# Row transfers by GpSimd in pairs, each pair waiting for the one before it to land

## The reference

```python
x = x + L0_conv(_gn(x))        # deformable 3x3 convolution
x = x + L1_conv(_gn(x))        # attention over the 1024 positions, 16-wide keys
t = _to_tokens(x)
t = t + L2_attn(_ln_t(t))      # attention with a distance bias
t = t + L2_ffn(_ln_t(t))       # mixture of 8 experts, top 2 of them
t = t + L3_attn(_ln_t(t))      # 16-head linear attention
t = t + L3_ffn(_ln_t(t))       # mixture of 8 experts, top 2 of them
```

```python
top2_vals, top2_idx = jax.lax.top_k(probs, 2)
...
h = gelu(xf @ w1 + bb1); y = h @ w2 + bb2
acc + we[:, None] * y
```

## Time and profile before

| | |
|---|---|
| median of 3 executions | 2342.63 us (2340.99 to 2352.11) |
| profiled execution, first to last instruction | 2532.1 us |
| mean granted TensorE clock in it | 0.883 of full speed |
| PE, DVE, ACT, POOL busy in it | 1926.7, 1494.0, 1039.0, 555.5 us |

### The profile page before, as it was taken

One profiled execution on the slowest core, in us unless ns is written; L12 is line 12 of the kernel. 1 busy time (PEld: TensorE's weight loads), 2 busy tenths in 40 slices (PEclk: granted clock), 3 DMA queues, 4 the chain that ended last, 5 costly groups with the idle time before them and its releaser, 6 DMA issues.

```text
span 2532.1 us, 35891 instructions
## 1 busy us (share of the span) xinstructions
PE 1926.7 (76%) x10992; PEld 1518.5 (60%) x10992; DVE 1494.0 (59%) x3449; ACT 1039.0 (41%) x1773; POOL 555.5 (22%) x535
## 2 busy tenths in 40 slices
PE   4777878887688777877778876786778877768749
PEld 1665656566556565756646665565656666556636
DVE  2356545876357754777447763577547864485363
ACT  3134144525363162733546253642627335443323
POOL 0000112021213323032222312133230422232020
PEclk7889989988899889988889888998889988888969
DMA  7901952474446734584455844476344844431410
GB/s 250 198 1 42 210 150 76 110 170 136 123 137 162 199 101 127 146 184 142 117 145 158 187 138 122 135 178 182 101 132 146 192 132 126 128 122 55 129 35 9
DMA packets 259912, 337.51 MB, mean 133 GB/s; under 512 B 29552, under 2 KB 191840, under 8 KB 259424
## 3 DMA queue, kind: packets, MB, share of 16 engines
q1 hardware_dynamic: 243648, 297.70, 44.7%
q0 software_dynamic: 14336, 29.39, 4.2%
q10 hardware_dynamic: 1696, 7.66, 0.8%
HBM read 267.56 MB, written 67.08 MB: 132 GB/s over the span
## 4 chain that ended last, share of the span: by engine, by line
PE 33%; issue 19%; DVE 18%; ACT 6%; DVEq 5%; DMA 5%; SPq 4%; another core or an unknown queue 4%; POOL 3%; ACTq 2%; PEld 0%; PEldq 0%; POOLq 0%
PE pair L948 5%; PE pair L1067 4%; POOL gotten L808 2%; PE pair L935 2%; PE pair L1235 2%; PE pair L1225 2%; PE pair L1115 2%; DMA dist<-hats 2%; PE pair L1127 2%; PE pair L1075 2%; DVE dist L1642 2%; PE pair L861 2%; PE pair L881 2%; DVE nmax L1751 1%
## 5 line engine op out<-in xcount | busy, mean ns | idle before, releaser
L948 PE MATMUL pair<-dist,thirds 128*128 128x256 f32 (+6 forms) x1440 | 299.2, 360 | 66.7 <-DVE dist L1642 60.7
L948 PEld LDWEIGHTS pair<-dist,thirds 128*128 128x128 f32 x1440 | 259.5, 205 | 115.3 <-DVE dist L1642 61.2
L1067 PE MATMUL pair<-vt,dist 128*128 128x128 f32 x2048 | 270.7, 288 | 37.3 <-DVEq L1745 32.9
L1067 PEld LDWEIGHTS pair<-vt,dist 128*128 128x128 f32 x2048 | 256.2, 202 | 60.5 <-DVEq L1745 49.8
L1433 ACT ACTIVATE hidden_sb<-pair,wring 128x128 f32<-128x128 f32 x644 | 184.3, 367 | 234.8 <-PE pair L1115 135.2
L808 POOL DMA_INDIRECT gotten<-ys,row x224 | 226.0, 1009 | 128.1 <-issue 65.8
L1115 PE MATMUL pair<-turned_sb,wring 128*128 128x128 f32 x1288 | 193.1, 295 | 65.1 <-DVEq L1796 37.2
L1127 PE MATMUL pair<-wring,hidden_sb 128*128 128x128 f32 x1288 | 184.5, 288 | 71.6 <-DVE tnF L1764 35.9
L1115 PEld LDWEIGHTS pair<-turned_sb,wring 128*128 128x128 f32 x1288 | 172.8, 205 | 106.6 <-DVEq L1796 61.9
L1642 DVE TENSOR_TENSOR dist<-dist,prob 128x1024 f32<-128x1024 f32 x144 | 173.9, 1224 | 95.7 <-DMA dist<-hats 46.9
L1127 PEld LDWEIGHTS pair<-wring,hidden_sb 128*128 128x128 f32 x1288 | 169.3, 202 | 81.7 <-issue 65.8
(11 more groups left out here) (256 smaller groups left out, 3162.0 us busy)
## 6 DMA issues: line engine op xcount, KB each, us to landing
dist<-hats SPq DMA_DIRECT2D x576, 128.0 KB
wring<-wa SPq DMA_DIRECT2D x161, 321.0 KB
wring<-wb SPq DMA_DIRECT2D x161, 321.0 KB
prob<-hats SPq DMA_DIRECT2D x288, 128.0 KB
hats<-dist SPq DMA_DIRECT2D x40, 512.0 KB, 3.9
ys<-by SPq DMA_DIRECT2D x70, 256.0 KB, 2.3
blocks_sb<-xs SPq DMA_DIRECT2D x28, 512.0 KB, 6.7
blocks_sb<-xs SPq DMA_DIRECT2D x14, 448.0 KB, 8.0
```

The source lines that it names most:

```text
L948: last = pe.matmul(pair[0][:, a:b], z[k // 3 % 2][:, c, k % 3, :], rhs(a, b), start=bank not in opened, stop=final, skip_group_check=True)
L1067: last = pe.matmul(psum[bank][:, 0:P], prT[j % 2][:, t, :], vt[:, t, :], start=(t == 0), stop=(t == NT - 1))
```

## The change

In `send` and `fetch` every part but the first now waits until all the parts before it have landed. With `part` counting from 0, each part before it has added 32 to the semaphore, hence the `32 * part`; `at(m, 256, ...)` counts the images before. And the last three parts of scatter A move from hooks 36, 44, 44 to 46, 47, 48, behind the `gn1` root at 45 and the second gating-B root at 46. No other table changes.

```diff
-SEND_A_AT = [28, 32, 34, 34, 36, 36, 44, 44]
+SEND_A_AT = [28, 32, 34, 34, 36, 46, 47, 48]
...
                 if part == 0:
                     pool.wait_ge(sem(f"routed{l}"), at(m, 1, 1))
                     pool.sem_inc(sem("moves_begun"), 1)
+                else:
+
+                    pool.wait_ge(sem(f"sent{l}"), at(m, 256, 32 * part))
                 tn = which(l)[3]
                 for r, j in MOVES[2 * part:2 * part + 2]:
                     pool.indirect_dma_start(xs[l], ...)
...
                     pool.sem_inc(sem("moves_begun"), 1)
+                else:
+
+                    pool.wait_ge(sem(f"got{l}"), at(m, 256, 32 * part))
                 for r, j in MOVES[2 * part:2 * part + 2]:
                     pool.indirect_dma_start(got[r][:, j, :], ...)
```

## The result

The changed kernel takes 2489.0 us at the median of 4 executions, the kernel before, run beside it on the same chip, 2345.07 us. The ratio is 1.0612, with a 95% interval of 1.0581 to 1.0642: **144 us slower**. The forecast was a rise of 58 us to 2401 us, with a range of 2320 to 2470 us. The direction was right; the size was not, and the time lies beyond the range.

What follows compares the result with a forecast made beforehand. The prediction took the kernel as bound by chains running from engine to engine, no engine being full. Its terms, 21 + 15 + 14 + 8 = 58 us, on 2342.6 us gave 2401 us, range 2320 to 2470 us.

Steps and rivals of the forecast that it cites:

- The price of one wait: In GpSimd's list, one wait on a landing adds 1.84 us, up to 3.60 us.
- Part one: Scatter A, group norm's root: TensorE's blocks 4.5 to 7.5 us late; 3 us in 7 periods, 21 us.
- Part two: Scatter B, second layer norm's root: GpSimd 3.3 us late without the stop; 2.5 us in 6 periods, 15 us.
- Part three: Gather A: VectorE's first settle waits 4.3 us without a stop; half let through, 2 us in 7 periods, 14 us.
- Part four: Gather B: ends far ahead of its use, covered by the convolution; costed at nothing.
- Part five: The end, behind the last period: less side work to fill a wait; 8 us, 26 us at most.
- The first: Rival: the stops are part of every execution and the pauses end them; 2241 us, chance 0.18.
- The second: Rival: everything is hidden by the covers; about 2343 us, within 0.5%, chance 0.14.
- The third: Rival: landings slow everywhere, each wait 3.60 us; 127 us more, 2470 us, chance 0.08.
- The stops: VectorE's waits ending with "remote" inside GpSimd's bursts, 159.3 us; taken to belong mostly to the profiled execution.

Runs made afterwards that it cites:

- experiment 2: Against the kernel before: waits only in scatter A, with its three pairs moved as in the changed kernel; 2378.59 us, ratio 1.0155.
- experiment 6: Against the kernel before: scatter A's three pairs moved, without any wait; 2359.11 us, ratio 1.0058.
- experiment 4: Against the kernel before: waits only in gather A, old order of steps; 2394.67 us, ratio 1.0206.
- experiment 8: Against the kernel before: waits only in the last five of the 28 bursts (35 waits), old order; 2390.81 us, ratio 1.0190.
- experiment 1: The kernel before, unchanged, run again for a second profile; 2345.42 us, ratio 1.0024, profiled span 2342.9 us.
- experiment 10: Against the kernel before: only every second pair waits (three waits a burst instead of seven), old order; 2365.79 us, ratio 1.0080.

## Why the direction was right and the size was not

**The mechanism** was right: pauses in GpSimd's list cost nothing by their sum, and they cost where another engine's step stands behind them. Every sign that the forecast named is in the profile after: pairs further apart (4.80 us in scatter B, forecast about 4.4), the group norm's root released by VectorE, a load of the blocks 13.0 us behind the second gating root (1149.75 to 1162.76; forecast about 12), TensorE's new wait for it, the second layer norm's root right behind a transfer, the first settle waiting for the gather.

**The price of one wait** was too low: 1.84 us was taken, 2.34 us is the mean, and it depends on the place: 13.4 us for six waits ahead of scatter B's root (1227.82 - 1196.78 against 1169.23 - 1151.64), 2.24 us each; 15.9 us for seven in gather A, 2.27 each; 3.3 us in gather B (3.6 - 0.3); 1.2 us in most waits of the last scatter (1.53 - 0.30). The forecast took the lower price "as most bursts stand in the attention stretches", as if these were quiet; scatter B and gather A stand there, and their waits are the 2.24 and 2.27 us. For the quiet stretch the sum was too high instead: landing and restart were added up to 1.29 + 0.85 = 2.14 us and took 1.53 us together. In the changed kernel the price goes with the traffic: the DMA share is 0.11 in the quiet last scatter (2274 to 2290), 0.48 and 0.52 in the scatter B and gather A shown, 0.91 in a gather B (1060 to 1111). That the traffic is the cause was not tested.

**Part one** forecast that TensorE finds the blocks 4.5 to 7.5 us late and let 3 us of it through: 21 us. The lateness was right (5.26 us in the period shown, 34.3 / 7 = 4.9 in experiment 2). The allowance for VectorE's slack was wrong: by itself the part cost 34 us, all of the lateness, and some 16 of them come with the move alone (experiment 6), for which the forecast's terms give 0 to 10 us. Beside the other waits TensorE's wait in the seven periods is 37.6 - 10.9 = 26.7 us.

**Part two** put 7.7 us of cover ahead of the root, once the stop was taken out; the second profile shows 7.54. The 15 us forecast stand against some 24 us of new waits in the periods (54.0 - 18.2 - 11.9), in five of them and not six: the dearer price.

**Part three** is the largest error in the periods. It found the gather 4.3 us late. The seven waits cost 15.9 instead of 12.9 us and the last landing took 2.59 instead of 1.29 (1287.34 to 1289.93), while the cover was 11.5 us and not 9.9: 15.9 + 2.6 - 11.5 = 7.0 us late, and VectorE waited 6.53 us there; experiment 4 alone has (60.8 - 10.8) / 6 = 8.3 us a period. And then half was let through "since VectorE has slack elsewhere". Of 60.8 us waited 50 came out at the end. 14 us were forecast, 50 measured for that gather, some 10 of them at the end.

**Part four** was right: gather B is all but free in the periods (2.0 us at the roots).

**Part five** is the largest error of all: 8 us, at most 26, against 44 (interval 32 to 58). It counted one scatter and one gather behind the last period; experiment 8 shows five places, each 8 to 12 us late, and little cover. The trace of before had them: the bursts of the last images could have been read one by one.

Together: 50 us forecast in the periods, 85 measured; 8 forecast at the end, 44 measured. The step that failed is not a wait that was overlooked in the periods but two allowances: in parts one and three about half of a lateness was written off, against the copy's 2.2 us and an average of busy time, where over 80% of gather A's wait came through; and in part five the end was taken as one lump of 8 us, at most 26, where five bursts cost 44 us. The price of a wait, 1.84 us for 2.34, added to both. The periods' 85 us lie within the 102 us that the bounds of parts one to three allow together; the end went 18 us beyond its own bound of 26. The two kernels add up to 129 us and not to 144; the intervals allow the difference, and it was not traced further.

**The rivals.** The first falls, with its premise: experiment 1 shows no stops. The second (everything hidden) fails at all places but gather B. The third, slow landings everywhere, had the nearest time, 2470 us, 19 us short; it came there by a price that is too high (3.60 us against 2.34) and with part one mostly let through, and its 20 us for the end are less than half of what was measured.

**The stops.** The rule of the page "NOTIFIC — the notification-queue block" of the Trainium skill (section 7.1) that was weighed, that a full record path holds the engine back, finds no support here: the second profile records as many instructions (35891) and has no stops. That it acted in the one execution behind the earlier trace rows can neither be shown nor excluded. Taking the stops out of that trace was the right step all the same: the cover in part two so found, 7.7 us, was the true one. The forecast also said that the profiled span might fall while the time rises. It did, but not because the pauses shorten the stops: the second profile of before has none to shorten, so that sign came true by luck.

## What to carry to other kernels

A wait on a landing, put into a queue of transfers, is priced at each place where another engine needs something from behind it: cover there against waits times their price in that stretch, and what is not covered is lost nearly whole; the mean busy share of an engine says nothing of its slack at that place. Read the last bursts one by one, since at the end of a pipeline little covers them: here 18% of the waits made 31% of the loss. If transfers have to be held apart, keep one pair in flight with a second semaphore (no measurable cost here), or put other work of the same queue between a pair and its wait: behind the root at 1227.85, which takes 1.03 us, the wait was 0.48 us, and that of the pair before it 1.53. Where several cheap waits fit the cover, as in experiment 10, they cost little too.

## What the runs showed beyond that

One execution of a kernel can be profiled in a condition that no other shows: 13 further profiles, one of them of the same kernel, have none of its stops. A profiled time that is 8% above the median should be taken again before anything is read off it.

TensorE's clock also falls around such a wait. Stretches of 4 us behind the first settle and around it, in the second profile of before and in the changed kernel (start and end; length, busy time of PE, PEld, DVE, ACT, POOL; PEclk, DMA share, GB/s):

```profile
1234.00:1238.00 4.00, 4.00 (x31) 3.47 (x30) 2.81 (x8) 2.68 (x8) 0.00 (x0) 1.00 0.71 195
```

```profile
1282.00:1286.00 4.00, 4.00 (x38) 3.96 (x36) 0.42 (x1) 3.04 (x7) 1.83 (x3) 1.00 0.67 190
1286.00:1290.00 4.00, 0.49 (x4) 0.10 (x2) 0.07 (x1) 3.42 (x8) 1.04 (x2) 0.84 0.66 194
1290.00:1294.00 4.00, 2.72 (x7) 1.86 (x8) 3.47 (x9) 2.59 (x5) 0.00 (x0) 0.50 0.29 120
1294.00:1298.00 4.00, 4.00 (x23) 2.87 (x22) 2.04 (x5) 0.26 (x1) 0.00 (x0) 0.80 0.00 0
1298.00:1302.00 4.00, 3.70 (x24) 2.69 (x23) 3.23 (x6) 3.30 (x6) 0.00 (x0) 1.00 0.02 4
```

Before, the granted clock is 1.00, its 2.4 GHz level, behind the settle. Now TensorE has almost nothing to do while VectorE waits; when the work comes back the granted clock is 0.50, the 1.2 GHz level, then 0.80, and 1.00 only in the third stretch. Over the whole kernel TensorE is busy 1901.9 us instead of 1871.6 us with the same 10992 instructions: 30 us more, of which the runs do not tell how much lies on the path that sets the end.
